# PSUM bank order inside the attention units, place of a weight fold, and order of the tail, in a six-layer Perceiver kernel

## What is computed

```python
x = x + gelu(ln(x) @ ctx.T) @ ctx            # context MLP, 4096 context rows a batch
x = x + latent_attention(ln(x))              # 8 heads
x = x + moe_ffn(ln(x))                       # 8 experts, top 2, width 688, and a shared one
energy = einsum('nqhd,nkhd->nhqk', heads(ln(x)), heads(ctx))     # 16 heads of 16, 4096 keys
x = x + softmax(where(mask, energy, -1e20) / 16) @ heads(ctx) @ w_out.T + b_out
query, keys, values = (unit(ln(x) @ W + b) for W, b in (q, k, v))  # f/(|f|+1e-8) in frequency
x = x + irfft(cumsum(rfft(keys) * rfft(values)) * conj(rfft(query)))
x = x + expert_attention(ln(x))              # 16 experts, gates, causal, head width 64
```

## Time and profile before

| | |
|---|---|
| median of 3 runs | 1061.0 us (1057.71 to 1061.58) |
| the profiled execution | 1053.22 us, span 1051.6 us |
| PE busy | 950.8 us (90%) |
| DVE busy | 596.9 us (57%) |
| ACT busy | 449.7 us (43%) |
| chain that ended last | PE 78%, DVE 7%, ACT 4%, DMA 4% |
| mean granted TensorE clock | 0.958 |

### The profile page before, as it was taken

One profiled execution on the slowest core, in us unless ns is written; L12 is line 12 of the kernel. 1 busy time (PEld: TensorE's weight loads), 2 busy tenths in 40 slices (PEclk: granted clock), 3 DMA queues, 4 the chain that ended last, 5 costly groups with the idle time before them and its releaser, 6 DMA issues.

```text
span 1051.6 us, 19842 instructions
## 1 busy us (share of the span) xinstructions
PE 950.8 (90%) x7080; PEld 547.2 (52%) x7080; DVE 596.9 (57%) x1539; ACT 449.7 (43%) x836; POOL 98.7 (9%) x135
## 2 busy tenths in 40 slices
PE   6999989969999995479999999999999999884887
PEld 5888865546566663224444444444444444463556
DVE  3445443643222222767777777777777777268683
ACT  3444424521122220246666666666666666532002
POOL 1322320003211111000000000000000000010000
PEclk9999996998999998689999999999999999997899
DMA  7744867034103443924455544455544461600000
GB/s 270 244 180 150 303 262 294 1 115 168 21 31 111 150 141 81 180 72 62 70 75 76 70 61 64 64 74 74 72 62 63 63 109 36 115 28 1 1 1 20
DMA packets 76315, 106.10 MB, mean 101 GB/s; under 512 B 27526, under 2 KB 62695, under 8 KB 72234
## 3 DMA queue, kind: packets, MB, share of 16 engines
q1 hardware_dynamic: 70866, 89.38, 38.4%
q0 software_dynamic: 5200, 15.61, 3.8%
q10 hardware_dynamic: 200, 0.44, 0.1%
HBM read 83.40 MB, written 20.22 MB: 99 GB/s over the span
## 4 chain that ended last, share of the span: by engine, by line
PE 78%; DVE 7%; ACT 4%; DMA 4%; issue 4%; SPq 2%; ACTq 0%; POOL 0%; POOLq 0%; DVEq 0%
PE bank L1295 13%; PE bank L1316 12%; PE bank L1304 9%; PE bank L1200 7%; PE bank L1273 5%; PE bank L1224 4%; PE bank L1007 3%; PE bank L994 3%; PE bank L1529 2%; ACT region L844 2%; PE bank L1173 2%; PE bank L1089 2%; PE bank L1327 2%; PE bank L1098 1%; PE bank L1588 1%
## 5 line engine op out<-in xcount | busy, mean ns | idle before, releaser
L844 ACT ACTIVATE region<-bank 128x512 f32<-128x512 f32 x512 | 278.0, 595 | 177.6 <-PE bank L1304 177.6
L1929 DVE CUSTOM_DVE_ANT_0 xnT<-bank,region 128x1024 bf16<-128x1024 f32 x128 | 156.2, 1220 | 89.3 <-issue 89.3
L1295 PE MATMUL bank<-region 128*128 (+1 forms) x1024 | 163.7, 277 | 13.9 <-ACT region L844 12.7
L1929 DVE CUSTOM_DVE_ANT_0 region<-bank,region 128x1024 bf16<-128x1024 f32 x128 | 156.3, 1221 | 0.4
L1295 PEld LDWEIGHTS bank<-region 128*128 128x128 bf16 x1024 | 68.2, 97 | 139.0 <-ACT region L844 61.5
L1316 PE MATMUL bank<-region 128*32 128x256 f32 x2048 | 138.9, 385 | 0.0
L1304 PE MATMUL bank<-region,identb 64*64 64x512 bf16 x1024 | 105.7, 403 | 0.0
L1273 PE MATMUL bank<-region,xnT 64*128 64x512 bf16 x248 | 75.7, 386 | 5.4 <-DMA xnT<-region 5.4
L1316 PEld LDWEIGHTS bank<-region 128*32 128x32 f32 x2048 | 58.9, 109 | 34.1 <-ACT region L844 14.3
L1200 PE MATMUL bank<-region 128*128 x240 | 74.9, 466 | 1.5 <-DVE region L1851 1.5
L1275 PE MATMUL bank<-region,xnT 64*128 64x512 bf16 x248 | 75.7, 386 | 0.0
(11 more groups left out here) (328 smaller groups left out, 1140.4 us busy)
## 6 DMA issues: line engine op xcount, KB each, us to landing
region<-keys_split SPq DMA_DIRECT2D x224, 128.0 KB, 4.9
region<-in_ctx SPq DMA_DIRECT2D x32, 512.0 KB, 4.3
keys_split<-region POOLq DMA_DIRECT2D x48, 256.0 KB, 4.0
region<-in_L_ffn_we_gate SPq DMA_DIRECT2D x8, 688.0 KB, 8.6
region<-in_L_ffn_we_up SPq DMA_DIRECT2D x8, 688.0 KB, 9.8
region<-in_L_ffn_we_down SPq DMA_DIRECT2D x8, 640.0 KB, 9.3
region<-in_mask_1x1xSxS_ik SPq DMA_DIRECT2D x1, 4096.0 KB, 16.3
mask_kept<-region SPq DMA_DIRECT2D x1, 2048.0 KB, 12.5
```

What stands on the lines that cost most here:

```text
L844: nc.scalar.activation(prob4[n % PROBS].rearrange("p a b -> p (a b)"), bank[:, SCORE4[n], :], ACT.Exp, scale=SCALE4).then_inc(exp4_ready, 1)
L1295: mm(bank[:, SCORE4[n], k * S:(k + 1) * S], slab[s][:, t * P:(t + 1) * P], qT4[:, bass.ds(u, 1), :].rearrange("p o q -> p (o q)"), start=( ...
L1929: v.tensor_tensor_reduce(out=junk[q], in0=bank[:, 3 + 2 * q:5 + 2 * q, :].rearrange("p a b -> p (a b)"), in1=maskN[:, q, 2 * c * CH:2 * (c ...
```

## The change

- `SCORE4` gives the score banks another order inside a unit, and the turned maximum goes to bank 1 (`NEG4`) instead of bank 0.
- The weight fold moves to the transition between the experts and stage 4. Its inputs are loaded in place of half of the second batch's context; PE folds behind the last expert block, ACT copies the result, SP stores it to DRAM and loads it again during stage 4. The eight context loads of the second batch are issued behind these stores.
- In unit 31 both projections of batch 0 stand behind the second group, and its normalised transpose and three spectra are made inside the unit. Bank numbers of stages 5 and 6 follow.
- DVE's list in stage 5 is written in another order, each reciprocal is a call of its own (`invert`), the gates of batch 0 stand behind `unbind(1)`, and those of batch 1 are cut in six pieces and placed between gathers 8 to 15. In stage 6 `mix(0)` is taken before the last two gathers, and `out_rows` is cut in parts around the transposes of the second batch.

```diff
--- before.py
+++ after.py
@@ -64,7 +64,8 @@
 NEG_ROWS = slice(32, 34)
 GROUPS = 8
 HALVES = 2 * GROUPS
-SCORE4 = (0, 1, 2, 0, 1, 2, 0, 1, 2, 0, 1, 2, 0, 1, 2, 1)
+SCORE4 = (0, 1, 2, 0, 1, 2, 0, 1, 0, 2, 1, 0, 2, 1, 0, 2)
+NEG4 = 1
 KT4 = CTX // P
 RING = 4
 MAXES = GROUPS
...
-DEEP6 = (5, 6, 0, 1, 2)
+DEEP6 = (5, 6, 2, 0, 1)
 HALF6 = QT * E6 // 2
 
 
-T5, Y5, SUM5, BROW5 = 4, 7, 2, 0
-FOLD5 = (5, 0, 5)
-SPEC5 = (5, 0)
+T5, Y5, SUM5, BROW5 = (3, 4), (4, 7), (2, 0), 0
+FOLD5 = (0, 2, 4)
+SPEC5 = (5, 3, 5, 0, 5, 0)
...
 
 N_CONST = 3
 N_FOLD2 = 8
 N_W2 = 9
-N_W5 = 10
...
@@ -537,8 +545,11 @@
                 if 2 * MOST3 <= i < 3 * MOST3:
                     load_mask(i - 2 * MOST3)
                 if i == 3 * MOST3:
-                    for c in range(4):
-                        load_ctx(1, c)
+                    for n, name in enumerate("kvq"):
+                        sp.dma_start(w5[:, n, :, :], a["L1_attn_W" + name].rearrange("(c p) n -> p c n", p=P)).then_inc(in_w5, 16)
+                        sp.dma_start(b5[:, n, :], a["L1_attn_b" + name].rearrange("(c p) -> p c", p=P),
+                                     allow_slow_non_contiguous=True).then_inc(in_w5, 16)
+                    sp.dma_start(dft, a["c_dft"].rearrange("(c p) n -> p c n", p=P)).then_inc(in_w5, 16)
             for s in range(XRING):
                 sp.wait_ge(y_stored[s], 16 * ((BLOCKS3 - s + XRING - 1) // XRING))
             for b in range(B):
@@ -551,11 +562,15 @@
                 sp.dma_start(slab[s][ONE_ROWS, :], ones_dram.broadcast_to([DH4, CTX])).then_inc(slab_ones, 16)
             for s in range(2, RING):
                 load_slab(s, s)
-            for c in range(4, 8):
-                load_ctx(1, c)
             sp.wait_ge(qT_ready, QT)
             for s in range(1, RING):
                 load_max_queries(s, s)
+            sp.wait_ge(fold_ready, 4)
+            sp.dma_start(fold_dram, fold_made.rearrange("p n c f -> p (n c f)")).then_inc(in_w5, 16)
+            sp.dma_start(brow_dram, brow_made[0:1, :, :].rearrange("p n f -> p (n f)")).then_inc(in_w5, 16)
+            sp.wait_ge(in_w5, 16 * N_W5[1])
+            for c in range(8):
+                load_ctx(1, c)
             sp.wait_ge(qT_ready, 2 * TT)
             sp.dma_start(bo4, a["L1_xattn_b_out"].partition_broadcast(P)).then_inc(in_wout, 16)
             with sp.Fori(0, U4 // RING - 1) as i:
@@ -566,10 +581,8 @@
                     load_max_queries(s, RING * i + s + RING)
 
             sp.wait_ge(v_ready, H4)
-            for n, name in enumerate("kvq"):
-                sp.dma_start(w5[:, n, :, :], a["L1_attn_W" + name].rearrange("(c p) n -> p c n", p=P)).then_inc(in_w5, 16)
-                sp.dma_start(b5[:, n, :], a["L1_attn_b" + name].rearrange("(c p) -> p c", p=P), allow_slow_non_contiguous=True).then_inc(in_w5, 16)
-            sp.dma_start(dft, a["c_dft"].rearrange("(c p) n -> p c n", p=P)).then_inc(in_w5, 16)
+            sp.dma_start(fold, fold_dram.rearrange("p (n c f) -> p n c f", n=3, c=DC)).then_inc(in_w5, 16)
+            sp.dma_start(brow, brow_dram.rearrange("o (n f) -> o n f", n=3).broadcast_to([P, 3, 2 * NF])).then_inc(in_w5, 16)
             sp.dma_start(idft[:, 0, :], a["c_idft"][0:P, :]).then_inc(in_w5, 16)
             sp.dma_start(idft[1:P, 1, :], a["c_idft"][P + 1:D, :]).then_inc(in_w5, 16)
...
@@ -799,6 +812,13 @@
                 nc.scalar.activation(hT3[0:FLAST, FT - 1, :], turned[0:FLAST, (FT - 1) * P:FT * P], ACT.Copy)\
                   .then_inc(hT_ready, 1)
 
+            for n in range(3):
+                act.wait_ge(fold_psum, n + 1)
+                nc.scalar.activation(fold_made[:, n, :, :], bank[:, FOLD5[n]:FOLD5[n] + 2, 0:2 * NF], ACT.Copy)\
+                  .then_inc(fold_ready, 1)
+            act.wait_ge(fold_psum, 4)
+            nc.scalar.activation(brow_made, bank[:, BROW5:BROW5 + 3, 0:2 * NF], ACT.Copy).then_inc(fold_ready, 1)
+
 
             for n in range(TT * 2):
                 t, half_h = TILE4[n]
...
@@ -838,8 +861,10 @@
                         o4T_out(0)
                     if n == 4 and not first:
                         sums_out(s - 1, u - 1)
-                    if n == 13 and last:
-                        fold_out(0)
+                    if n == 10 and last:
+                        batch_norm_out(3, 0, T5[0])
+                    if n == 14 and last:
+                        squares(0)
                     act.wait_ge(score4, HALVES * u + n + 1)
                     nc.scalar.activation(prob4[n % PROBS].rearrange("p a b -> p (a b)"), bank[:, SCORE4[n], :],
                                          ACT.Exp, scale=SCALE4).then_inc(exp4_ready, 1)
@@ -850,28 +875,11 @@
                     softmax_numerators(s, RING * i + s)
             for s in range(RING):
                 softmax_numerators(s, U4 - RING + s, last=(s == RING - 1))
-            batch_norm_out(3, 0)
+            squares(1)
             sums_out(RING - 1, U4 - 1)
-            fold_out(1)
+            squares(2)
             act.wait_ge(in_gate, 16 * DC + 32)
...
@@ -1244,6 +1266,15 @@
                     rows_T(i + 1)
                 hidden_T(i)
             down_rows(BLOCKS3 - 1, before)
+
+            pe.wait_ge(in_w5, 16 * N_W5[0])
+            for n in range(3):
+                fold_weights(n)
+            pe.wait_ge(fold_ready, 2)
+            for n in range(3):
+                last = fold_bias(n)
+            last.then_inc(fold_psum, 1)
+            pe.wait_ge(fold_ready, 4)
 
 
             def queries_T(n):
...
+
+            def last_unit(j, whole):
+
+                if j == 0 and whole:
+                    y4_rows(0, 0)
+                    y4_rows(0, 1)
+                elif j == 2 and not whole:
+                    batch_norm_T(xn5[0], 6, T5[0])
+                elif j == 2:
+                    pe.wait_ge(in_w5, 16 * N_W5[2])
+                    pe.wait_ge(xnT_ready, 4)
+                    spectra(0)
+                    spectra(1)
+                elif j == 3 and whole:
+                    spectra(2)
 
             for n in range(TT):
...
@@ -1449,42 +1484,23 @@
             unit(RING - 1, U4 - 1, U4 // RING, False, 0, last_unit)
             for g in range(GROUPS - 2, GROUPS):
                 values_group(RING - 1, U4 - 1, g)
-            fold_weights(1)
             sum_rows(RING - 1, U4 - 1).then_inc(oT_psum, 1)
-            pe.wait_ge(fold_ready, 1)
-            fold_weights(2)
-            pe.wait_ge(xnT_ready, 4)
-            o4_T(1)
-            pe.wait_ge(fold_ready, 2)
-            fold_bias(0)
-            for q in range(QT):
-                y4_rows(1, q)
-            fold_bias(1)
-            fold_bias(2).then_inc(fold_psum, 1)
             pe.wait_ge(sim_sq, 1)
+            pe.wait_ge(spec_ready, 2)
             for c in range(DC):
                 last = mm(bank[:, 3, NORM6:NORM6 + E6], ones[:, :], sim2[:, c, :], start=(c == 0), stop=(c == DC - 1),
...
-            dve.wait_ge(fold_ready, 4)
             spectrum_out(0)
             spectrum_out(1)
             magnitude(0)
             bind(0)
             magnitude(1)
             spectrum_out(2)
-            inverse_sizes(0)
+            rows_out(0, U4 - 2)
+            rows_out(None, U4 - 1)
+            dve.wait_ge(norm6_psum, 1)
+            v.tensor_copy(square6[:, TT:TT + E6], bank[:, 3, NORM6:NORM6 + E6]).then_inc(pow_arg, 1)
+            magnitude(2)
+            dve.wait_ge(gate_exp, 1)
+            link(v.tensor_scalar(col6[:, 2, :], col6[:, 0, :], 1.0, None, ALU.add))
+            link(v.reciprocal(col6[:, 3, :], col6[:, 2, :]))
+            key_sizes(0)
+            invert(1, 0)
             scale_keys(0)
+            dve.wait_ge(y4_psum, TT)
+            add_psum(1, Y5[1])
+            layer_stats(halves[1])
+            query_sizes(0)
+            layer_scale(6, halves[1], xn5[1])
+            invert(2, 0)
...
@@ -2116,55 +2152,75 @@
             link(v.reciprocal(root6[:, TT:], root6[:, TT:]))
             spectrum_out(5)
             add_inverse(0)
-            inverse_sizes(1)
+            key_sizes(1)
             layer_scale(7, halves[0])
+            invert(1, 1)
             scale_keys(1)
             magnitude(5)
-
-            def gates(b):
-
-                ts = halves[b]
...
@@ -2227,33 +2283,62 @@
                 dve.wait_ge(y6_psum, max(t + 1, QT))
                 v.tensor_tensor(x[:, t, :], x[:, t, :], bank[:, OUT6[b][q], q * D:(q + 1) * D], ALU.add).then_inc(x_final, 1)
 
-            unit_queries(1)
-            gates(0)
-            unbind(1)
+            gate_logits(0)
+            gate_best(0, logit, first)
+            gate_rest(0)
+            gate_best(0, eq, second)
+            gate_active(0)
+            gate_arguments(0)
+            gate_shares(0)
             for k in range(4):
                 gather(k)
             add_inverse(1)
             gather(4)
             layer_scale(8, halves[1])
-            for k in range(5, HALF6):
+            for k in range(5, 9):
                 gather(k)
```

(16 more changed lines are left out.)

358 lines of the change are left out of this document (188 added, 170 removed).

## The result

The changed kernel takes 1022.9 us (median of 4 runs, 1018.9 to 1027.3) against 1059.4 us (4 runs, 1054.4 to 1061.6): a ratio of 0.969, 95% interval [0.965, 0.973], so 36.4 us less. The forecast was 36.4 us less and 1024.6 us. Its profiled execution took 1018.9 us, of which 1017.2 are the span; before it was 1053.2 and 1051.6, so the two traces differ by 34.4 us of span.

The account below looks back on a forecast made before the run. PE was taken to bound the kernel (90% busy), with waits for ACT in units, for query copies before them, and DVE's pace behind them. Terms -15.2 - 4.2 - 11.0 - 4.6 - 1.4 = -36.4 gave 1024.6 us, range 1015 to 1036.

Parts of the forecast that it names:

- Bank order: Units 0 to 30: PE's wait for ACT at half 15 goes, 0.49 us a unit, -15.2 us.
- The rival that nothing is gained: Units: a new wait of 0.49 us at half 8 or half 0 cancels the bank order's gain; 1039.8 us, chance 0.09.
- the slower one: Units: waits at both half 8 and half 0 cost 2.0 us a unit; about 1087 us, chance 0.04.
- Transition: Before the first unit: queries' copies go ahead of context loads and the fold is covered; first unit near 450.15, -4.2 us.
- The reason I gave for SP being harmless: SP's queue: stores land by 450, context loads near 468, unit 4's slab is used at 488; slack 14 us, no cost.
- The bound of full clock: First unit: -2.9 us if PE ran it at 2.4 GHz; the forecast counted no gain.
- The rival of -2.9: First unit keeps the full clock because PE idles less before it; sum -39.3, 1021.7 us, chance 0.18.
- Last unit and stage 5 to the first gather: From the last unit's start, DVE is the chain after the last sums; first gather at 63.95 instead of 74.9, -11.0 us.
- First gather to last projection: Tail: new places of DVE's other work and gates(1) in pieces; 45.95 us against 50.6, -4.6 us.
- my second rival: The tail gives back 8 to 10 us through a 1.2 GHz clock or hand-overs; 1033 to 1035 us, chance 0.18.
- End: After the last projection: mix(0) no longer waits for the last gathers, out_rows fills waits; 24.7 us against 26.1, -1.4.
- terms 3 to 5: Last unit to the end: -11.0 to the first gather, -4.6 to the last projection, -1.4 at the end.

Follow-up runs that it names:

- the two pairs: New bank order alone in the kernel before (1037.2 us against 1059.4), and old bank order in the changed kernel (1034.9 us against 1022.9).
- the experiment at half 14: Changed kernel with a bank order in which half 14 reuses the bank of half 12: 1030.2 us, ratio 0.975 to the kernel before.
- the two versions with norm 9 early: Changed kernel with DVE adding inverse(1) ahead of all gathers and scaling batch 1's last norm after one: 1015.8 us; with 37 useless PE matmuls too: 1018.7 us.
- context first: Changed kernel with SP's stores, the wait for them and four context loads ahead of the copies of queries: 1030.3 us, ratio 0.976 to the kernel before.
- the version with gates ahead of unbinding: Changed kernel with batch 0's gates on DVE back ahead of the unbinding of batch 1: 1020.0 us, ratio 0.969 to the kernel before.
- fillers: 37 matmuls of no use to the result, put in PE's idle places: 1021.9 us in the changed kernel, 1018.7 us with batch 1's last norm early too.

## Why the prediction was right

1. **Bank order**, forecast -15.2: measured -15.5 and -15.4 in the two pairs, and a period of 13.83 us against 13.82. The slack of half 15 is 0.16 us (0.17 forecast); half 0 starts at 617.09, and exponential 14, which starts at 616.13, ends 0.42 us ahead of it (0.4 forecast). Half 8 starts at 610.42, 0.91 us behind the end of exponential 6 (0.9 forecast). The rival that nothing is gained and the slower one both fell. That short slacks are a real danger is shown by the experiment at half 14, where 0.1 us are lacking and each unit pays 0.23.

2. **Transition**, forecast -4.2: -4.7 by the first stretch and -4.4 from the first matmul for the maxima on; -4.8 and -4.0 in the kernel before with only the queue's order changed. The first unit starts at 450.85, forecast 450.15, and the experts' part was 1.2 us later in this execution. (The forecast's own steps, 448.3 + 1.22 + 0.28 + 0.15, add up to 449.95; 0.2 us are without a step.) The fold costs nothing, as forecast, even done twice. The reason I gave for SP being harmless held: I had the stores landed by 450, and SP went on at 450.38. But I had named that time without working it out; the landing took 13.3 us from the issue of the second store, and 17.3 in the other order, and with the queries behind it it cost 8 us.

 The bound of full clock: unit 0 began at 0.50 to 0.52 until 454 us and ran at 1.00 from then on, where before it stayed at 0.50 to about 460. POOL's first sum of rows comes 17.66 us after the unit's start (468.51) where it was 19.23 (473.54); about 0.5 of that is the bank order's, so my "no gain" was wrong by about 1 us (the middle stretches of kernels with the same bank order say 0.7 to 0.8: 445.7 against 444.9, 430.2 against 429.5). The rival of -2.9 did not come in the profiled execution. In the two versions with norm 9 early, whose transition is the same code, that stretch is another 1.1 us shorter at a clock of 0.80 and 1.00 in 450.5 to 454. So the same code finds either clock, and the whole matter is worth about 2 us. The rule drawn on in the prediction (the Trainium skill, "TensorE: Matmul & The Clock Gate", section "The HAM clock gate", that activity releases the throttle) agrees in direction with these rows, not with a firm -2.9.

3. **Last unit and stage 5 to the first gather**, forecast 63.95 after the last unit's start: 64.5. The last sums are at 22.7 (22.65); the step that slipped is the spectrum ahead of unbinding(0), which I priced at the full clock: 40.3 against 39.3, of which 0.4 was made up by the first gather. Against before this is -10.4 instead of -11.0.

4. **First gather to last projection**, forecast 45.95: 48.1. This is the term that was mis-sized most, by 2.2 us. The order of events is as forecast (PE idle 4.78 us ahead of norm 9, forecast 5; 1.17 us at heads_T(0), forecast 1.4). But I had priced what comes behind norm 9 at the full clock. All of the slip lies there: 40.9 us from norm 9 to the last projection, where the forecast has 109.9 - 71.25 = 38.65. The clock was 0.66 behind PE's idle 4.78 us, so that the transposes of norm 9 took 1.11 us instead of 0.60 and the eight matmuls (two projections) behind them 4.00 instead of 2.75. That is 1.7 of the 2.2 us, and the version with gates ahead of unbinding, which has the full clock there, takes 39.2 us. It was my second rival's mechanism, a low clock behind PE's idle time, at a small part of the 8 to 10 us that I gave it. The other 0.5 us stays open.

5. **End**, forecast 24.7: 24.2 (993.01 to 1017.2), so -1.9 against before instead of -1.4. Against before, term 4 is -2.4 instead of -4.6, and terms 3 to 5 together are -14.8 instead of -17.0. Their parts have experiments for the place of the spectra and the gates, but no run takes the new order of the last unit or of the end alone.

The sum in spans: +1.2 for the experts' later end, then -4.7, -16.1 and -14.8 give -34.4; the forecast was 0, -4.2, -15.2 and -17.0, or -36.4. Of the 2.0 us between them the tail lacked 2.2 and the experts took 1.2, while the transition and the units gave 0.5 and 0.9 more than forecast. That the medians differ by exactly the 36.4 us of the forecast is luck: they scatter by several us.

## What to carry to other kernels

With three banks in rotation, the distance that counts is not how many halves lie between two uses but how much of PE's other work does: put the short reuses behind blocks of PE's work that don't write score banks (here the values), and compute the slack of each from the timeline. A place that stops PE for 0.3 us in the record can cost 0.49 in each unit. Small transfers that an engine waits for go ahead of bulk loads in their queue, and a queue that must wait for its own stores does so behind everything urgent. When PE idles in a tail for work of DVE, look at what DVE does ahead of it that nobody needs yet (here four gathers, 2.5 to 4.5 us).

## What the runs showed of the hardware that I had not expected

- Two stores (774 KB and 3 KB) behind 28 slab loads of 128 KB landed only 13.3 us (changed kernel) and 17.3 us (context first) after the second was issued, and SP, which waits for them, issues nothing in that time. Four context loads of 512 KB took SP 9.05 us to issue right behind the slabs, and 2.06 us behind that wait.
- From the end of ACT's exponential to PE's first matmul in the freed bank it was 0.10 us in one kernel (612.13 to 612.23) and 0.06 in another (711.57 to 711.63, and the earlier trace rows).
- The same code is granted different clocks at the same place: 0.72 in one execution and 1.00 in another at the fourth spectrum, 0.52 and 1.00 in unit 0, 0.99 and 0.64 at the projections behind norm 8 (935 to 942 us). Each such place is worth 1 to 2 us here, and holding the clock with fillers took away as much as it gave.
